# Second attention: which of a batch's 128 score tiles have their row sums taken by ScalarE, cut from 22 to 13

## The chip, the cores and the metric

One core of one Trainium2 chip runs the whole kernel. The metric is the device time of one execution in microseconds (us), the median of several runs; lower is better.

## What is computed

Two transformer-like blocks over x of shape (4, 1024, 128). The first has an attention with softmax over negative Euclidean distances and a mixture of experts. The change touches only the second block:

```python
xn = layernorm(x)
q, k, v = split(xn @ w_in.T + b_in)          # 16 heads of width 8
att = softmax(einsum('blhd,bmhd->blmh', q, k) / sqrt(8), axis=2)
opt = einsum('blmh,blhd->blhd', att, v)      # v is weighted by the sum of its own row of att
x = x + opt @ w_out.T + b_out + sqrt(real**2 + imag**2)   # real, imag: xn @ cos(..), xn @ sin(..)
```

So of every 1024 x 1024 score matrix the kernel needs only exp of each entry and the sum of each row.

## The kernel before, in words

The kernel has two long stages. In the first (to 996 us) the first attention and the experts run. In the second, from 996 us to the end, there are 4 batches x 16 heads x 8 row blocks = 512 score tiles of 128 rows x 1024 columns, 128 of them in a batch. A tile has a number s from 0 to 127 in its batch; `n` is its head counted over all batches and `i` its row block. Below, "tile 81" is s = 81.

Each tile goes through three engines.

- TensorE (PE) makes the scores into one of `RING` = 3 buffers of PSUM (`scores1`, L1211). It may fill a buffer when the exp of the tile three earlier has released it.
- ScalarE (ACT) takes exp of the tile into SBUF (`act_exp1`). There are 8 such places, in 4 tensors of two (`EX`), so tile s uses the place of tile s - 8. Before the exp of an even tile, ACT waits for the semaphore `summed` (L1226), until VectorE has folded every tile up to s - 7.
- The row sum of the tile is made in one of two ways. Mostly VectorE (DVE) does a fold (`dve_fold`, L1244): it adds the left and right half of the tile and writes out the row sum as an accumulator. For tiles for which `sum_by_act` is true, ACT makes the sum as part of the exp (`accum_out`, L1232, followed by a read of its accumulator), and DVE has nothing to do for that tile beyond waiting for its exp. The others are L1236.

`sum_by_act` before the change is true in batches 0 to 2 for s = 16, 21, 26, ..., 121, that is 22 tiles of a batch, and for the last two row blocks of the last four heads of batch 3 (8 tiles).

Beside its folds DVE does other work at fixed places of a batch. All of it stands in one queue, written out by hand in `fast(dve)`, so each item waits for everything ahead of it:

- s = 30: add the attention output (L1067); 31 to 38 and 39 to 46: one add per tile (L1074, L1083); 40: L1298
- 47 to 54 statistics (L1091); 55 variance; 57 to 64 normalise (L1099)
- 72: copy of the transposed tokens (L1114)
- 81: q out of PSUM (`dve_keep_q1`, L1128). GpSimd (POOL) waits for this and then splits q into three bf16 parts with four instructions (L520, L522, L524, L526)
- 90: k out of PSUM (`dve_keep_k1`, L1137). It releases the PSUM buffer `aux`, for which PE's value product waits (`pe_value1`, L1156, in PE's queue behind the scores of tile 97)
- 92, 94, 96, 98: DVE's own split of k (L1143, L1147, L1149, L1151)
- 100: the values out of PSUM (`dve_keep_v1`, L1165). This releases `aux` again; the first mix product waits for it (`pe_mix`, L1171, in PE's queue behind the scores of tile 108)
- 31, 63, 95, 127: the weights of four heads (`dve_weigh`, L1254 to L1259)

PE's queue is in order too, so the scores of tile 98 stand behind the value product's first part, and those of tile 109 behind the mix product's.
At tile 26, and in batches 1 to 3 at tile 36, PE puts four bias matmuls of 512 columns (L1047) between the scores of that tile and of the next.

Of the kernel before, what the change touches and what calls it, by code (L numbers as in the profile page):

```python
# [27 lines left out]
H = 16  # L28
HD = D // H
NT = N // P  # L30
HEADS = B * H
GROUP = 4
# [41 lines left out]


LAST_PARTS = [(0, 4), (4, 6), (6, 8)]


def sum_by_act(n, i):
    s = n % H * NT + i  # L80
    return n < HEADS - H and 12 <= s < 124 and s % 5 == 1 or n >= HEADS - GROUP and i >= LAST_PARTS[-1][0]

# [4 lines left out]
def tile_at(b, s):  # L89
    if b < B - 1 or s < LAST_GROUP:  # L90
        return b * H + s // NT, s % NT
    s -= LAST_GROUP
    lo, hi = next((lo, hi) for lo, hi in LAST_PARTS if s < GROUP * hi)
    head, i = divmod(s - GROUP * lo, hi - lo)
# [4 lines left out]
for tile_number in range(HEADS * NT):  # L99
    FOLDS.append(FOLDS[-1] + (not sum_by_act(*tile_at(*divmod(tile_number, H * NT)))))  # L100
# [85 lines left out]
def build(nc, d):  # L186
    with ExitStack() as ctx, ExitStack() as scores_ctx, ExitStack() as room:
# [1033 lines left out]
        def act_exp1(act, o, b, s):  # L1221
            (n, i), k = tile_at(b, s), s % NT
            tile = o.filled(act, ("qk1", n, i))
            if n:
                if k % 2 == 0:
                    act.wait_ge(summed, FOLDS[b * H * NT + s - NT + 2])  # L1226
            elif i == 0:
                act.wait_ge(pv_done, CHG * (GROUPS - 1) + CH)
            if sum_by_act(n, i):
                if n >= 2 * GROUP:  # L1230
                    act.wait_ge(w_done, n // GROUP - 1)
                nc.scalar.activation(EX[k // 2][:, k % 2, :], tile, ACT.Exp, scale=SCALE1,  # L1232
                                     accum_out=den[n // GROUP % 2][:, n % GROUP, i:i + 1]
                                     ).then_inc(o.release(("qk1", n, i)), 1)
            else:
                nc.scalar.activation(EX[k // 2][:, k % 2, :], tile, ACT.Exp, scale=SCALE1  # L1236
                                     ).then_inc(o.release(("qk1", n, i)), 1)

        def dve_fold(dve, o, b, s):
            (n, i), k = tile_at(b, s), s % NT  # L1240
            o.emptied(dve, ("qk1", n, i))
            if not sum_by_act(n, i):
                tile = EX[k // 2]
                nc.vector.scalar_tensor_tensor(  # L1244
                    out=tile[:, k % 2, 0:N // 2], in0=tile[:, k % 2, 0:N // 2], scalar=1.0,
                    in1=tile[:, k % 2, N // 2:N], op0=ALU.mult, op1=ALU.add,
                    accum_out=den[n // GROUP % 2][:, n % GROUP, i:i + 1]).then_inc(summed, 1)

        def dve_weigh(dve, u, part, number, sums_ready, count):

            side, b, blocks = u % 2, u // PER_BATCH, slice(*part)
            weights, sums_of = wsum[side][:, :, blocks], den[side][:, :, blocks]
            dve.wait_ge(sums_ready, count)
            nc.vector.reciprocal(weights, sums_of).then_inc(inv_done, 1)  # L1254
            dve.wait_ge(inv_done, number)
            nc.vector.tensor_tensor(weights, weights, sums_of, ALU.mult).then_inc(w_done, 1)
            dve.wait_ge(w_done, number)
            vals = V1[b][:, blocks, u % PER_BATCH * 32:(u % PER_BATCH + 1) * 32].rearrange("p t (h e) -> p t h e", e=HD)
            nc.vector.tensor_tensor(vals, vals, bcast(weights.rearrange("p h t -> p t h"), 3, HD), ALU.mult  # L1259
                                    ).then_inc(weighed, 1)  # L1260

        def dve_weigh_last(dve, number):
            lo, hi = LAST_PARTS[number]
            dve_weigh(dve, GROUPS - 1, (lo, hi), GROUPS + number, summed,
                      FOLDS[(B - 1) * H * NT + LAST_GROUP + GROUP * hi])
# [37 lines left out]
        def pe_turn_last(pe, o, number, slot):  # L1303
            lo, hi = LAST_PARTS[number]
            tile = o.begin(pe, ("fturn", B - 1, number), slot)
            pe.wait_ge(weighed, PER_BATCH * B + number)
            for t in range(lo, hi):
                mm = nc.tensor.transpose(tile[:, (t - lo) * P:(t - lo + 1) * P], V1[B - 1][:, t, :], ident)
                if t == hi - 3:
                    yield  # L1310
            mm.then_inc(o.fills(("fturn", B - 1, number)), 1)
            yield

        def dve_keep_last(dve, o, number):
            lo, hi = LAST_PARTS[number]
            tile = o.filled(dve, ("fturn", B - 1, number))
            nc.vector.tensor_copy(fatt[:, lo * P:hi * P], tile[:, 0:(hi - lo) * P]
                                  ).then_inc(o.release(("fturn", B - 1, number)), 1)

        def pe_project_last(pe, o, number, slot):  # L1320
            lo, hi = LAST_PARTS[number]
            tile = o.begin(pe, ("fwo", B - 1, number), slot)
            add_bias(tile, "bo1", hi - lo)
            yield
            o.emptied(pe, ("fturn", B - 1, number))
            for t in range(lo, hi):
                mm = nc.tensor.matmul(tile[:, (t - lo) * P:(t - lo + 1) * P], fatt[:, t * P:(t + 1) * P], late["wo1"],
                                      start=False, stop=(t == hi - 1))
                if t < hi - 1:
                    yield  # L1330
            mm.then_inc(o.fills(("fwo", B - 1, number)), 1)
            yield
# [984 lines left out]
```

## Time and profile before

| | us |
|---|---|
| median of 3 runs | 1486.84 |
| lowest and highest of them | 1486.05, 1487.32 |
| the profiled execution, as timed | 1486.19 |
| its span, first to last instruction | 1484.5 |
| second stage, from 996 us to the end | 488 |
| exp of tiles, ACT | 512 instructions |

The second stage begins at 996.2 us, and its batches begin at 996.2, 1114.8, 1234.2 and 1353.6 us. Batches 0, 1 and 2 follow the same pattern to within hundredths of a microsecond in the part that the argument uses, so one of them, batch 1, is read in detail. In the timeline views, each line is a merged group: start of the first instruction, microseconds from there to the end of the last, and what it is. ACT's instructions overlap in the trace (the next is shown as started before the one ahead has ended), so distances are best taken from end to end.

### The profile page before, as it was taken

How to read it: one execution, taken by the hardware profiler on the slowest of the kernel's cores; microseconds unless marked ns; L12 is line 12 of the kernel's file. 1: busy time of each engine (PE TensorE's matmuls, PEld its weight loads, DVE VectorE, ACT ScalarE, POOL GpSimd, SP SyncE). 2: the span in 40 equal slices, each digit the busy share in tenths (PEclk: the TensorE clock that was granted, in tenths of full speed). 3: DMA queues.
4: the chain of work that ended last, by engine and by line, in shares of the span. 5: the costliest groups of instructions: out<-in, count | busy, mean ns of one | idle time of the engine just before them, and what ended most of it. 6: DMA issues, size and time to landing. Idle time of an engine off the chain costs nothing.

```text
span 1484.5 us, 21370 instructions
## 1 busy us (share of the span) xinstructions
PE 1121.4 (76%) x7881; PEld 441.7 (30%) x7910; DVE 1245.5 (84%) x2236; ACT 1450.1 (98%) x792; POOL 413.7 (28%) x305
## 2 busy tenths in 40 slices
PE   5587786887887978878878774777677677776666
PEld 2123223243252442433424411232123222222212
DVE  7997978988989889789797787858898898988786
ACT  4899999999999999999999999999999999999998
POOL 5184460655503302123022130032123024022200
PEclk8598988999999999999999987899999999999999
DMA  4842644223242112121121420134033133021020
GB/s 130 240 131 61 177 127 124 52 57 84 79 135 69 51 43 53 43 56 52 43 66 30 95 74 18 32 107 87 27 112 84 27 112 83 27 91 48 21 70 20
DMA packets 104059, 112.71 MB, mean 76 GB/s; under 512 B 41722, under 2 KB 76026, under 8 KB 103946
## 3 DMA queue, kind: packets, MB, share of 16 engines
q1 hardware_dynamic: 98618, 99.47, 24.7%
q0 software_dynamic: 4464, 11.09, 2.7%
q8 instruction: 66, 1.08, 0.3%
q10 hardware_dynamic: 864, 0.69, 0.2%
q14 instruction: 47, 0.39, 0.1%
HBM read 66.52 MB, written 44.70 MB: 75 GB/s over the span
## 4 chain that ended last, share of the span: by engine, by line
ACT 69%; DVE 17%; issue 7%; PE 7%; DMA 1%; SPq 0%; DVEq 0%; ACTq 0%
ACT scores L719 25%; ACT scores L708 23%; ACT exp L1236 13%; DVE exp L1244 7%; DVE scores L683 6%; ACT exp L1232 3%; PE pvb L664 2%; ACT ht L969 1%; PE ring L649 1%; ACT L719 1%; ACT L708 1%; PE ring L426 1%; PE ring L930 1%; PE ring L1211 0%; DMA limit_full<-in_limit_full 0%
## 5 line engine op out<-in xcount | busy, mean ns | idle before, releaser
L683 DVE TENSOR_SCALAR scores<-ring 128x1024 f32<-128x1024 f32 x512 | 589.6, 1215 | 31.5 <-PE ring L649 31.3
L719 ACT ACTIVATE scores<-scores 128x8192 f32<-128x8192 f32 x64 | 445.8, 7021 | 0.2
L1236 ACT ACTIVATE exp<-ring 128x1024 f32<-128x1024 f32 x438 | 431.4, 1398 | 0.2
L708 ACT ACTIVATE scores<-scores 128x8192 f32<-128x8192 f32 x60 | 417.1, 7020 | 0.7 <-DVE scores L683 0.6
L1211 PE MATMUL ring<-stk 128*128 128x512 bf16 x995 | 299.5, 384 | 128.3 <-ACT exp L1236 106.6
L664 PE MATMUL pvb<-scores,val 128*9 128x256 f32 x4096 | 325.2, 392 | 89.9 <-ACT scores L719 44.0
L1244 DVE SCALAR_TENSOR_TENSOR exp<-exp 128x512 f32<-128x512 f32 x438 | 321.8, 757 | 62.1 <-ACT exp L1236 57.8
L649 PE MATMUL ring<-stk 64*128 64x512 bf16 x1024 | 210.3, 408 | 54.6 <-DVE scores L683 43.5
L1211 PEld LDWEIGHTS ring<-stk 128*128 128x128 bf16 x1024 | 65.7, 97 | 338.1 <-ACT exp L1236 241.8
L649 PEld LDWEIGHTS ring<-stk 64*128 64x128 bf16 x1024 | 49.8, 93 | 287.3 <-DVE scores L683 199.1
L664 PEld LDWEIGHTS pvb<-scores,val 128*9 128x9 f32 x4096 | 65.5, 89 | 219.4 <-issue 215.4
L704 POOL DMA_DIRECT2D att<-attg x32 | 25.2, 790 | 344.0 <-DVE attg L697 343.2
L1232 ACT ACTIVATE exp<-ring 128x1024 f32<-128x1024 f32 x74 | 101.1, 1369 | 0.2 <-PE ring L1211 0.2
L974 POOL TENSOR_TENSOR ht<-ht,gate 128x2464 f32<-128x2464 f32 x10 | 54.6, 5462 | 146.4 <-ACT ht L969 146.4
L930 PE MATMUL ring<-w,xjt 128*128 (+1 forms) x280 | 86.9, 469 | 1.2 <-DVE xjt L957 1.2
L672 PE MATMUL pvb<-fixed_full,ot 128*128 128x128 f32 x128 | 30.2, 320 | 55.0 <-DVE ot L688 55.0
L930 PEld LDWEIGHTS ring<-w,xjt 128*128 128x128 f32 x280 | 53.6, 195 | 30.2 <-issue 1.9
L976 POOL TENSOR_TENSOR gate<-gate,ht 128x2464 f32<-128x2464 f32 x10 | 54.6, 5457 | 0.8
L950 PE MATMUL ring<-w,ht 128*128 128x128 f32 (+3 forms) x420 | 49.4, 276 | 4.5 <-DVE ht L981 4.5
L950 PEld LDWEIGHTS ring<-w,ht 128*128 128x128 f32 (+1 forms) x420 | 47.7, 191 | 6.7 <-issue 4.2
L987 DVE COPY yj<-ring 128x896 f32<-128x896 f32 x10 | 10.9, 1092 | 42.0 <-PE ring L950 42.0
L962 DVE COPY ht<-ring 128x352 f32<-128x352 f32 x70 | 36.7, 525 | 10.9 <-PE ring L930 4.0
(252 smaller groups left out, 1178.8 us busy)
## 6 DMA issues: line engine op xcount, KB each, us to landing
stk<-stack SPq DMA_DIRECT2D x192, 192.0 KB, 2.9
stack<-qp SPq DMA_DIRECT2D x7, 768.0 KB, 4.4
stack<-kp SPq DMA_DIRECT2D x7, 768.0 KB, 5.7
xj<-xg SPq DMA_DIRECT2D x10, 448.0 KB, 4.2
yg<-yj POOLq DMA_DIRECT2D x10, 448.0 KB, 3.6
stack<-qp SPq DMA_DIRECT2D x7, 512.0 KB, 5.1
stack<-kp SPq DMA_DIRECT2D x7, 512.0 KB, 5.1
stk<-sum_rows SPq DMA_DIRECT2D x128, 24.0 KB
```

Source lines behind the costliest of these rows:

```text
L649: mm = nc.tensor.matmul(tile[:, cols], stk0[slot][side, K, j * P:(j + 1) * P], stk0[slot][side, Q, cols], start=True, stop=True)
L664: mm = nc.tensor.matmul(pvb[place % 2][32 * c:32 * c + VW, 0:256], val[place][:, j, :], S[place][:, j * N + c * 256:j * N + (c + 1) * 256] ...
L683: nc.vector.tensor_scalar(S[place][:, j * N:(j + 1) * N], tile, 1e-12, None, ALU.max).then_inc(o.release(("qk", group, place, j)), 1)
L708: nc.scalar.activation(S[place][:], S[place][:], ACT.Sqrt).then_inc(root_done, 1)
L719: nc.scalar.activation(S[place][:], S[place][:], ACT.Exp, scale=-1.0).then_inc(exp_done, 1)
L930: mm = nc.tensor.matmul(tile[:, side * 512:side * 512 + I], xjt[:, j * P:(j + 1) * P], weights_of(w13, e[j])[:, :, side, :].rearrange("p o ...
L950: mm = nc.tensor.matmul(tile[:, j * P:(j + 1) * P], ht[0:width, j, c * P:(c + 1) * P], weights_of(w2, e[j])[0:width, :, c, :].rearrange("p ...
L974: nc.gpsimd.tensor_tensor(h1, h1, gate[:, :, :], ALU.mult).then_inc(part_done, 1)
L1211: mm = nc.tensor.matmul(out[:, cols], stk1[place][:, Q, i * P:(i + 1) * P], stk1[place][:, K, cols], start=True, stop=True)
L1232: nc.scalar.activation(EX[k // 2][:, k % 2, :], tile, ACT.Exp, scale=SCALE1, accum_out=den[n // GROUP % 2][:, n % GROUP, i:i + 1]).then_in ...
L1236: nc.scalar.activation(EX[k // 2][:, k % 2, :], tile, ACT.Exp, scale=SCALE1).then_inc(o.release(("qk1", n, i)), 1)
L1244: nc.vector.scalar_tensor_tensor(out=tile[:, k % 2, 0:N // 2], in0=tile[:, k % 2, 0:N // 2], scalar=1.0, in1=tile[:, k % 2, N // 2:N], op0 ...
```

## The change

The rule of every fifth tile now holds only for tiles in three stretches of a batch. Of the 22 tiles of a batch (0 to 2) that ACT summed, 9 go to DVE: 31, 36, 41 (between 28 and 44) and 66, 71, 76, 81, 86, 91 (between 62 and 94). 13 stay with ACT. Over three batches 27 row sums move. The counts for which ACT and DVE wait (`FOLDS`) are computed from the same function and follow. Batch 3 is not changed, and nothing else moves.

```diff
 LAST_PARTS = [(0, 4), (4, 6), (6, 8)]
+DENSE = [(12, 28), (44, 62), (94, 124)]


 def sum_by_act(n, i):
     s = n % H * NT + i
-    return n < HEADS - H and 12 <= s < 124 and s % 5 == 1 or n >= HEADS - GROUP and i >= LAST_PARTS[-1][0]
+    dense = any(lo <= s < hi for lo, hi in DENSE)
+    return n < HEADS - H and dense and s % 5 == 1 or n >= HEADS - GROUP and i >= LAST_PARTS[-1][0]
```

## Rows read from the trace of the kernel before

**Rows 1.** The page: span, and busy time and share of each engine.
```profile
span 1484.5 us, 21370 instructions
PE 1121.4 (76%) x7881; PEld 441.7 (30%) x7910; DVE 1245.5 (84%) x2236; ACT 1450.1 (98%) x792; POOL 413.7 (28%) x305
```

**Rows 2.** ACT in order of time, batch 3, tiles summed by DVE only.
```profile
1412.12 56.14 ACT L1236 ACTIVATE exp<-ring 128x1024 f32<-128x1024 f32 x61
...
1412.12 2.06 ACT L1236 ACTIVATE exp<-ring 128x1024 f32<-128x1024 f32 x2
```

**Rows 3.** ACT in order of time, batch 1, tiles 81 to 86.
```profile
1190.47 1.46 ACT L1232 ACTIVATE exp<-ring 128x1024 f32<-128x1024 f32 x1
...
1191.47 4.21 ACT L1236 ACTIVATE exp<-ring 128x1024 f32<-128x1024 f32 x4
1195.09 1.51 ACT L1232 ACTIVATE exp<-ring 128x1024 f32<-128x1024 f32 x1
```

**Rows 4.** ACT, tiles 36 and 37 of batch 1, then of batch 3.
```profile
1148.73 1.10 ACT L1232 ACTIVATE exp<-ring 128x1024 f32<-128x1024 f32 x1
...
1149.93 1.02 ACT L1236 ACTIVATE exp<-ring 128x1024 f32<-128x1024 f32 x1
...
1393.47 1.25 ACT L1236 ACTIVATE exp<-ring 128x1024 f32<-128x1024 f32 x1
...
1394.82 1.02 ACT L1236 ACTIVATE exp<-ring 128x1024 f32<-128x1024 f32 x1
```

**Rows 5.** DVE in order of time, batch 1: folds of tiles 45 and 47.
```profile
1158.76 0.70 DVE L1244 SCALAR_TENSOR_TENSOR exp<-exp 128x512 f32<-128x512 f32 x1
...
1160.32 0.69 DVE L1244 SCALAR_TENSOR_TENSOR exp<-exp 128x512 f32<-128x512 f32 x1 [0.32 <-ACT exp L1236]
```

**Rows 6.** DVE, batch 1: q (tile 81), folds of tiles 83, 87 and 88.
```profile
1192.05 1.28 DVE L1128 TENSOR_SCALAR ysh<-aux,late_full 128x1024 f32<-128x1024 f32 x1 [0.30 <-ACT exp L1232]
...
1193.88 1.49 DVE L1244 SCALAR_TENSOR_TENSOR exp<-exp 128x512 f32<-128x512 f32 x1
...
1199.28 2.60 DVE L1244 SCALAR_TENSOR_TENSOR exp<-exp 128x512 f32<-128x512 f32 x1
...
1201.82 0.68 DVE L1244 SCALAR_TENSOR_TENSOR exp<-exp 128x512 f32<-128x512 f32 x1
```

**Rows 7.** POOL in order of time: first and last of the four splits of q.
```profile
1193.40 1.43 POOL L520 CAST qp<-ysh 128x1024 bf16<-128x1024 f32 x1 [22.46 <-DVE ysh L1128]
...
1198.88 2.45 POOL L526 TENSOR_TENSOR qp<-ysh,qp 128x1024 bf16<-128x1024 f32 x1
```

**Rows 8.** DVE, batch 1: k (tile 90), fold of tile 99, values (tile 100).
```profile
1203.65 1.27 DVE L1137 TENSOR_SCALAR yro<-aux,late_full 128x1024 f32<-128x1024 f32 x1
...
1213.06 0.69 DVE L1244 SCALAR_TENSOR_TENSOR exp<-exp 128x512 f32<-128x512 f32 x1
...
1214.28 1.23 DVE L1165 TENSOR_TENSOR V<-aux,late_rows 128x1024 f32<-128x1024 f32 x1
```

**Rows 9.** Stretches of batch 1: microseconds, DVE busy, granted clock, DMA.
```profile
1192.05:1201.82 9.77, 9.77 (x12) 1.00 0.07 22
1201.82:1213.06 11.24, 11.14 (x28) 1.00 0.44 158
```

**Rows 10.** ACT in order of time, batch 1: tiles 105, 106 and 108 with 109.
```profile
1212.64 1.70 ACT L1236 ACTIVATE exp<-ring 128x1024 f32<-128x1024 f32 x1
1213.84 1.42 ACT L1232 ACTIVATE exp<-ring 128x1024 f32<-128x1024 f32 x1
...
1215.76 2.33 ACT L1236 ACTIVATE exp<-ring 128x1024 f32<-128x1024 f32 x2
```

**Rows 11.** PE, batch 1: first value product, scores of tile 98, first mix product.
```profile
1204.98 0.71 PE L1156 MATMUL aux<-late_full,att_t 128*128 128x128 f32 x4 [0.23 <-DVE yro L1137]
1205.53 0.59 PE L1211 MATMUL ring<-stk 128*128 128x512 bf16 x2
...
1215.56 0.70 PE L1171 MATMUL aux<-cs,att_t 128*128 128x256 f32 x2 [0.56 <-DVE V L1165]
```

## The prediction

> **What bounds the kernel now.** I read the page first: ACT is busy 98% of the span, DVE 84% [rows 1]. That is an average, so next I read ACT in order of time where the change acts. In batch 3 61 exps in a row run without ACT summing anything. From the end of the second to the end of the last are 56.14 - 2.06 = 54.08 us for 59 steps, 0.9166 us each [rows 2]. ACT is back to back, and this is its pace. In batch 1 the exp of tile 81, which ACT sums, ends at 1190.47 + 1.46 = 1191.93 and that of tile 86, the next such, at 1196.60 [rows 3]: 4.67 us for five steps, against 5 x 0.9166 = 4.58. So **a row sum made by ACT costs 0.08 us**, and it falls behind the tile (the four exps between have their last end at 1195.68, 3.75 us after tile 81, where 4 steps are 3.67). The rest of the work of the stage is hidden behind this pace as long as PE and DVE keep up. Starts run ahead of ends in these rows, so a start that slips shows a gap and costs nothing until it comes later than 0.10 us before the end of the exp ahead. I take that bound from an exp started late, which takes 1.02 us [rows 4]: with 1.02 - 0.92 = 0.10 of overlap the pace still holds.
>
> The second thing to read is how far DVE is behind, because ACT may not write tile s (even) before tile s - 7 is folded. A fold takes 0.61 us from start to start when DVE is behind: from the fold of tile 99 over that of tile 100 to the values, 1213.06 to 1214.28 for two [rows 8]. In most of a batch DVE is quicker than ACT's pace. Between tiles 82 and 105 it isn't.
>
> **What the change removes.** 27 sums of ACT, nine in each of batches 0 to 2, at 0.08 us. One place gives nothing: tile 36 in batches 1 and 2. There the next exp waits for PE, which has bias matmuls to do. With ACT summing tile 36 (batch 1) the ends of 36 and 37 are 1149.83 and 1150.95, 1.12 us apart; in batch 3, where ACT doesn't sum it, they are 1394.72 and 1395.84, the same 1.12 us [rows 4]. So 25 sums pay: before tile 81 six in batch 0 (0.49 us), five in batches 1 and 2 (0.41 us each). Tiles 81, 86 and 91 I account for below, with what follows.
>
> **What it adds before tile 81: nothing.** Between 28 and 46 DVE has an add per tile beside its folds. Fold 45 starts at 1158.76, 0.39 us after its exp is there. With three more folds (3 x 0.61) and an ACT that is 3 x 0.08 us earlier it starts 0.39 + 1.83 + 0.24 = 2.5 us late. ACT would be held from 4.6 us on: the exp seven steps on ends 7 x 0.917 = 6.42 us after this one and starts 1.02 before its end, and a fold's sum is out 0.78 after its start (step 4), 6.42 - 1.02 - 0.78. After that, DVE is idle from time to time (0.32 us ahead of fold 47 [rows 5]) and skips tiles 46, 51, 56 and 61, so it has caught up before the normalisation at 57, and PE's transposes at 68 see it on time. The folds of 66, 71 and 76 go into idle time: today DVE waits for ACT before each next fold. Cover gone, each would cost 0.61 us.
>
> **From tile 81 to tile 109: the loss.** Let T be the end of exp 81 (1191.93 today).
> 1. *The q copy moves.* Today DVE takes q out at 1192.05, T + 0.12 [rows 6]. Now fold 81 stands ahead of it: it starts at T + 0.03 and the copy 0.61 later, T + 0.65. That is 0.53 us later. POOL waits for this copy: its four splits run from 1193.40 to 1201.33 [rows 7] and start 0.53 us later too.
> 2. *DVE crawls meanwhile.* During these 8 us DVE does one fold per POOL instruction: folds 83, 84, 85 and 87 start between 1193.88 and 1199.28 and two of them take 2.60 us; the next starts at 1201.82 [rows 6]. Without POOL four folds are 2.4 us. The pattern starts from the q copy, so I let it move as a whole, with 86 as the fourth fold in place of 87.
> 3. *Two more folds in the backlog.* 86 and 91 each push what follows by 0.61. So all DVE work from fold 92 on is 0.53 + 1.22 = 1.76 us later, counted from T. There is no idle time to take it: DVE is busy 9.77 of 9.77 us and then 11.14 of 11.24 [rows 9].
> 4. *ACT is held.* Fold 99 starts today at 1213.06, T + 21.13 [rows 8], and exp 106 starts right when its sum is out, 1213.84, 0.78 later, while exp 105 ends only at 1214.34 [rows 10]: the wait is there today, and free by 0.4 us. In the new kernel fold 99 starts at T + 22.89 and exp 106 at T + 23.67; it ends at T + 24.69 and exp 109, three steps and one ACT sum on, at T + 27.52.
> 5. *The same by another way.* The values leave PSUM today at 1215.51 [rows 8], the mix product has waited for that by 0.56 us [rows 11], and exp 109 starts at 1216.73, 1.22 after (the pair 108 and 109 ends at 1218.09 [rows 10]). In the new kernel the values are out at T + 25.34, exp 109 starts at T + 26.56 and ends at T + 27.58. Two waits agree to 0.06; I take the later one.
> Today exp 109 ends at T + 26.16. **The new kernel is 1.42 us later there**, and the two sums of 86 and 91 and that of 81 are already in it. On the way there are smaller holds (tile 94: fold 87 starts at T + 10.41 instead of being done; tile 98, below), and these are absorbed: the later wait sets the time.
>
> After tile 109 DVE skips 111, 116 and 121 as today and catches up, and the loads of the next batch's first head are not near the edge. Batch 3 has no changed tile.
>
> **The sum.** Batch 0: +1.42 - 0.49 = +0.93. Batches 1 and 2: +1.42 - 0.41 = +1.01 each. Together +2.96 us. The profiled execution has a span of 1484.5 and a time of 1486.19; it becomes 1487.5 and 1489.1. The median of the runs, 0.65 above that execution, becomes **1489.8**. Anything under 0.2% (3.0 us) can't be told from no change here, so the forecast stands just on that line, on the slow side of the old kernel.
>
> **The rule of the skill that promises a gain.** The trace shows ACT at 98% and everything else well below [rows 1]. The Trainium skill ("Perfetto Trace Analysis", Identifying the Most-Contended Engine) says to find the engine with the highest occupancy and relieve that one; by that rule this change should win. The rows on DVE between 82 and 106 speak against it: there DVE, not ACT, is the engine without slack. What the rule gives is the first rival.
>
> **Rivals.**
> - *Gain: the eight places of exps take up the backlog.* Then only the 25 paying sums count: 25 x 0.08 = 2.0 us less, 1484.8. The point from which it decides is fold 99: with exp 105 ending at T + 22.16, it must start by T + 21.28, and today it starts at T + 21.13. So 0.15 us of added backlog is free, and a single fold is 0.61. It would need idle time that rows 9 don't show. 0.06.
> - *The q copy's move costs nothing*, because POOL's splits catch a fold less or the pattern shifts into place. Then 1.22 instead of 1.76: per batch 1.42 - 0.53 = 0.89, and the sum is 3 x 0.89 - 1.31 = +1.4, 1488.2. 0.14.
> - *PE's wait adds up.* The value product waits 0.23 us for the k copy today [rows 11]; that copy (1203.65 [rows 8]) is 1.14 us later after folds 81 and 86. The scores of tile 98 are then made at T + 15.3 (today 1206.12, T + 14.2), where exp 98 should start at T + 14.9 at the latest. This 0.4 us is absorbed in my sum; if it isn't, 3 x 0.4 is on top: 1491.0. 0.14.
> - *A fold more is caught in each POOL chain.* A caught fold takes up to 2.54 us from start to start instead of 0.61 (1199.28 to 1201.82 [rows 6]): 3 x 1.9 on top, 1495.6. For it: the chain starts later against ACT, with DVE further behind. Against: there are four POOL instructions, and each lets one fold through. 0.07. The Trainium skill ("SBUF — State Buffer", Who interferes with whom) names the cause, one port pair held for a whole instruction by whichever of VectorE and GpSimd starts first, while the other fully blocks. The durations in rows 6 and 7 agree; the rule doesn't say who goes first after the move.
>
> **How the numbers follow.** The forecast has 0.59. Its own spread is 0.7 us (0.65 between profiled execution and median is the size of the scatter, and batches repeat to hundredths). Half of it lies over the line of 3.0 us. Slower: 0.30 + 0.14 + 0.07 = 0.51. Same: the other 0.29, and 0.14 + 0.06 with the gain rival, whose 0.13% is within the line: 0.49. Faster by over 0.2% would need more than all 27 sums give (2.2 us), so I take only 0.02 for it out of the 0.49. Range: the forecast and its two neighbours, 1487.7 to 1491.4, which holds 0.87 less their outer tails, about 0.8. Outside are the gain and the caught fold.
>
> **What would show it.** Right: exps of L1232 39 + 8 instead of 66 + 8; folds of L1244 465 instead of 438; the four POOL splits of batch 1 start 2.0 us after exp 81's end instead of 1.5; ACT starts near tiles 94, 98, 104 and 106 with an exp of 1.02 us behind a gap; tile 81 to 109 takes 27.6 us from end to end instead of 26.2; PE's wait ahead of L1156 above 1 us. Wrong: exps from 94 to 106 without gaps (gain), a q split that hasn't moved, or five folds of more than a microsecond between the q copy and tile 90.

## The result, and the profile after

| | before | after |
|---|---|---|
| median, us | 1486.84 | 1492.58 |
| lowest to highest of 7 runs | 1486.05 to 1487.49 | 1491.43 to 1492.88 |
| the profiled execution, as timed | 1486.19 | 1492.79 |
| its span | 1484.5 | 1491.1 |

The ratio is 1.0035, with a 95% interval of 1.0026 to 1.0044. The kernel became 5.7 us slower. The forecast was 3.0 us slower (1489.8) with a range up to 1491.4, so the direction was right, the size was about half of the measured one, and the measured time lies above the range.

The page of the changed kernel, in the lines that answer to [rows 1], and its groups of exps and folds:

```profile
span 1491.1 us, 21395 instructions
...
PE 1130.5 (76%) x7910; PEld 445.0 (30%) x7910; DVE 1260.0 (84%) x2290; ACT 1449.1 (97%) x765; POOL 414.5 (28%) x305
...
L1238 ACT ACTIVATE exp<-ring 128x1024 f32<-128x1024 f32 x465 | 438.3, 1310 | 5.2 <-PE ring L1213 3.7
...
L1246 DVE SCALAR_TENSOR_TENSOR exp<-exp 128x512 f32<-128x512 f32 x465 | 339.4, 752 | 55.3 <-ACT exp L1238 49.0
...
L1234 ACT ACTIVATE exp<-ring 128x1024 f32<-128x1024 f32 x47 | 56.6, 1207 | 1.2 <-PE ring L1213 0.8
```

27 sums have moved (465 folds, 47 sums of ACT). Line numbers are two higher than before. What is new is idle time of ACT ahead of its exps, 5.2 and 1.2 us, and its largest releaser is PE, not DVE. The kernel before shows 0.2 and 0.2 us:

```profile
L1236 ACT ACTIVATE exp<-ring 128x1024 f32<-128x1024 f32 x438 | 431.4, 1398 | 0.2
...
L1232 ACT ACTIVATE exp<-ring 128x1024 f32<-128x1024 f32 x74 | 101.1, 1369 | 0.2 <-PE ring L1211 0.2
```

**Where the time goes.** I compare the end of each exp with the same exp in the kernel before, counted from the end of the batch's first exp. The table gives the changed kernel less the one before in microseconds, for tile 112 and for four points on the way; a minus means that the changed kernel is ahead.

| up to the end of exp | batch 0 | batch 1 | batch 2 |
|---|---|---|---|
| 81 | -0.48 | -0.41 | -0.40 |
| 93 | -0.73 | -0.65 | -0.65 |
| 99 | +1.62 | +0.08 | +1.71 |
| 109 | +1.62 | +1.10 | +1.70 |
| 112 | +1.62 | +1.83 | +1.70 |

The three batches lose 5.15 us together. Nothing more is lost between tile 112 and the end of a batch, and batch 3 is as before. The profiled execution has another 0.94 us ahead of the second stage. In a second trace of the same kernel the second stage starts 0.66 us earlier than before, so that part is scatter between executions: over the twelve traces of this document, whose kernels are the same up to there, the stage starts between 995.2 and 997.4 us. The last 0.5 us of the difference in span (6.6 us) falls behind the last exp. Those are the last four matmuls of the kernel before, and of the changed one:

```profile
1481.08 0.71 PE L1327 MATMUL ring<-late_full,fatt 128*128 128x128 f32 x4
...
1487.19 1.19 PE L1329 MATMUL ring<-late_full,fatt 128*128 128x128 f32 x4
```

In the changed kernel the granted clock (the share of TensorE's full clock that it is given) is at 0.50 there, from 1486.6 us on; in the kernel before it falls at 1482.4 us, when PE is done. Seven of the twelve traces have 5.7 to 6.0 us behind the last exp and five 5.3 to 5.4; e7_quiet_sums below, the fastest kernel, is one of the seven. So this part stays out of the batch figures.

**What came out as forecast.** Below is DVE of the changed kernel in order of time, batch 1: q, folds 83, 86, 87 and 99, values. T, the end of exp 81, is 1194.09 here.

```profile
1194.74 1.28 DVE L1130 TENSOR_SCALAR ysh<-aux,late_full 128x1024 f32<-128x1024 f32 x1
...
1196.55 1.51 DVE L1246 SCALAR_TENSOR_TENSOR exp<-exp 128x512 f32<-128x512 f32 x1
...
1201.97 2.60 DVE L1246 SCALAR_TENSOR_TENSOR exp<-exp 128x512 f32<-128x512 f32 x1
...
1204.50 0.68 DVE L1246 SCALAR_TENSOR_TENSOR exp<-exp 128x512 f32<-128x512 f32 x1
...
1216.97 0.68 DVE L1246 SCALAR_TENSOR_TENSOR exp<-exp 128x512 f32<-128x512 f32 x1
...
1218.19 1.22 DVE L1167 TENSOR_TENSOR V<-aux,late_rows 128x1024 f32<-128x1024 f32 x1
```

And POOL's first split of q, then ACT's exps of tiles 106 and 109, of the same batch:

```profile
1196.09 1.43 POOL L522 CAST qp<-ysh 128x1024 bf16<-128x1024 f32 x1 [22.75 <-DVE ysh L1130]
...
1217.74 1.02 ACT L1234 ACTIVATE exp<-ring 128x1024 f32<-128x1024 f32 x1 [0.41 <-issue]
...
1220.72 1.02 ACT L1238 ACTIVATE exp<-ring 128x1024 f32<-128x1024 f32 x1
```

The q copy starts at T + 0.65 (1194.74 - 1194.09), the first split at T + 2.00, fold 87 at T + 10.41, fold 99 at T + 22.88, and the exps of 106 and 109 at T + 23.65 and T + 26.63. The prediction had 0.65, 2.0, 10.41, 22.89, 23.67 and 26.56. In batches 0 and 2 DVE's items stand at the same distances from T, fold 99 at 22.88 in both. In batch 1 tiles 81 to 109 take 27.66 us from end to end (forecast 27.6, before 26.2).

**What didn't.** In batch 1 another 0.73 us goes between tiles 109 and 112, and in batches 0 and 2 the whole loss comes by tiles 98 and 99. There exp 106 starts at T + 24.33 and T + 24.34, 0.7 us later than DVE's fold 99 would let it (T + 23.67), so in these two batches it isn't DVE's wait that sets the time. These are ACT's rows of tiles 98 and 99 in batch 0 and of tile 111 in batch 1:

```profile
1089.34 1.02 ACT L1238 ACTIVATE exp<-ring 128x1024 f32<-128x1024 f32 x1 [1.25 <-PE ring L1213]
...
1090.94 1.02 ACT L1238 ACTIVATE exp<-ring 128x1024 f32<-128x1024 f32 x1 [0.58 <-PE ring L1213]
...
1223.28 1.02 ACT L1234 ACTIVATE exp<-ring 128x1024 f32<-128x1024 f32 x1 [0.62 <-PE ring L1213]
```

All three wait for PE. PE in batch 0, in order of time, at the place of [rows 11]:

```profile
1087.23 1.22 PE L1158 MATMUL aux<-late_full,att_t 128*128 128x128 f32 x4 [1.31 <-DVE yro L1139]
1088.24 1.06 PE L1213 MATMUL ring<-stk 128*128 128x512 bf16 x2
1089.10 1.06 PE L1158 MATMUL aux<-late_full,att_t 128*128 128x128 f32 x4
...
1090.74 0.61 PE L1158 MATMUL aux<-late_full,att_t 128*128 128x128 f32 x4
```

PE waits 1.31 us for DVE's k copy (0.23 before), and then each group of four value matmuls takes 1.22 and 1.06 us where [rows 11] have 0.71, and 0.61 again from 1090.74 on. The stretches of 3.4 us at that place, in batches 0, 1 and 2, say why. The columns after the time are busy time (and instructions) of PE, PE's weight loads, DVE, ACT and POOL, then the granted TensorE clock, the DMA share and GB/s.

```profile
1085.30:1087.30 2.00, 0.67 (x3) 0.18 (x3) 2.00 (x6) 2.00 (x4) 0.00 (x0) 0.99 0.99 379
1087.30:1090.70 3.40, 3.40 (x12) 2.63 (x13) 3.40 (x10) 1.82 (x2) 0.00 (x0) 0.50 0.69 266
...
1220.40:1223.80 3.40, 3.40 (x9) 1.77 (x8) 3.40 (x13) 2.74 (x4) 0.00 (x0) 0.50 0.62 207
...
1329.60:1333.00 3.40, 3.40 (x13) 2.52 (x14) 3.40 (x10) 1.74 (x2) 0.00 (x0) 0.50 0.70 269
```

**The granted clock is at 0.50, that is 1.2 GHz instead of 2.4, for 3.4 us in each of the three batches**, right behind a stretch in which PE was busy for a third of the time or little more (0.67 of 2.00 us, 0.94 of 2.40, 0.69 of 2.00). In the kernel before it stays at 1.00 throughout batches 0 to 2 ([rows 9] show two of its stretches). A fall isn't new to it, though: in batch 3 it has one of 6.8 us from 1373.2 on, and the ends of exps 17 to 19, which lie in it, are 0.91 to 0.92 us apart, ACT's pace. The changed kernel has 10.2 us there, and its exps of batch 3 are those of the kernel before to 0.01 us. The slow stretch falls on the value product in batches 0 and 2 and on the mix product in batch 1, which is just where ACT loses time that the forecast doesn't have.

### The profile page after: what moved, and what is told of

The parts are those of the page before. It is cut to its first block, busy times and chain, and to the rows that moved or that the text cites. A ratio compares the mean times of both kernels' runs of the same rounds, so it can differ in the third digit from the quotient of the medians.

```text
span 1491.1 us, 21395 instructions
## 1 busy us (share of the span) xinstructions
PE 1130.5 (76%) x7910; PEld 445.0 (30%) x7910; DVE 1260.0 (84%) x2290; ACT 1449.1 (97%) x765; POOL 414.5 (28%) x305
## 4 chain that ended last, share of the span: by engine, by line
ACT 72%; issue 11%; DVE 10%; PE 3%; POOL 2%; DMA 1%; SPq 0%; DVEq 0%; ACTq 0%; POOLq 0%
ACT scores L721 28%; ACT scores L710 27%; ACT exp L1238 12%; DVE exp L1246 4%; DVE scores L685 4%; ACT ht L971 1%; ACT exp L1234 1%; ACT L721 1%; ACT L710 1%; POOL yro L1025 1%; PE ring L428 1%; PE pvb L666 1%; PE ring L1213 1%; DMA x<-in_x 0%; PE ring L651 0%
## 5 line engine op out<-in xcount | busy, mean ns | idle before, releaser
L1238 ACT ACTIVATE exp<-ring 128x1024 f32<-128x1024 f32 x465 | 438.3, 1310 | 5.2 <-PE ring L1213 3.7
L1213 PE MATMUL ring<-stk 128*128 128x512 bf16 x1024 | 308.5, 388 | 120.6 <-ACT exp L1238 106.2
L1246 DVE SCALAR_TENSOR_TENSOR exp<-exp 128x512 f32<-128x512 f32 x465 | 339.4, 752 | 55.3 <-ACT exp L1238 49.0
L1234 ACT ACTIVATE exp<-ring 128x1024 f32<-128x1024 f32 x47 | 56.6, 1207 | 1.2 <-PE ring L1213 0.8
L1188 POOL TENSOR_TENSOR at<-at 128x1024 f32<-128x1024 f32 x8 | 17.4, 2175 | 102.1 <-DVE at L1184 102.1
```

The lines of the kernel that those rows point to most:

```text
L1213: mm = nc.tensor.matmul(out[:, cols], stk1[place][:, Q, i * P:(i + 1) * P], stk1[place][:, K, cols], start=True, stop=True)
L1246: nc.vector.scalar_tensor_tensor(out=tile[:, k % 2, 0:N // 2], in0=tile[:, k % 2, 0:N // 2], scalar=1.0, in1=tile[:, k % 2, N // 2:N], op0 ...
```

## The experiments

The theory after the result: the loss has two parts, DVE's backlog as forecast (3 us), and a fall of TensorE's clock (2 us), brought about by ACT's holds and PE's waits for DVE. The rivals: the backlog alone costs 5 us, and the clock is harmless or chance; or the early sums cost something too.

Each kernel was timed in 5 to 11 executions, against executions of the kernel before. The edits below are against the changed kernel. The summary is in one table, with the ratio of the times and its 95% interval, and batch figures as above (end of exp 112, less the kernel before, from one trace of each kernel); a star marks a batch in which the clock fell between tiles 94 and 112.

| kernel | median, us (before) | ratio, interval | batches 0, 1, 2 |
|---|---|---|---|
| changed | 1492.58 (1486.84) | 1.0035 (1.0026 to 1.0044) | 1.62*, 1.83*, 1.70* |
| e0_again | 1492.24 (1487.16) | 1.0038 (1.0024 to 1.0051) | 1.75*, 2.09*, 1.50* |
| e1_late_sums | 1493.73 (1487.16) | 1.0043 (1.0029 to 1.0057) | 2.01*, 2.58*, 1.42 |
| e2_early_sums | 1486.35 (1487.16) | 0.9993 (0.9984 to 1.0002) | -0.23, -0.41, -0.41 |
| e3_pe_later | 1492.86 (1487.16) | 1.0035 (1.0022 to 1.0049) | 0.89*, 0.96, 0.96 |
| e9_pe_later2 | 1489.07 (1486.69) | 1.0016 (1.0007 to 1.0025) | 0.88, 0.96, 1.16* |
| e4_pe_waits | 1488.19 (1486.69) | 1.0011 (1.0002 to 1.0020) | 0.25, 0.26, 0.25 |
| e6_no81 | 1491.50 (1486.69) | 1.0027 (1.0018 to 1.0037) | 1.71*, 0.88, 2.04* |
| e10_pe_busy | 1490.02 (1486.88) | 1.0020 (1.0011 to 1.0029) | 1.04, 1.03, 1.03 |
| e7_quiet_sums | 1483.71 (1486.69) | 0.9979 (0.9970 to 0.9988) | -0.70, -0.73, -0.73 |
| e8_early_q | 1485.93 (1486.88) | 0.9991 (0.9982 to 1.0000) | -0.34, -0.26, -0.27 |

**The changed kernel again (e0_again).** No edit.

> The changed kernel once more, for a second trace. Theory (DVE backlog and TensorE clock): each of batches 0 to 2 again loses 1.6 to 1.8 us from its first exp to that of tile 112, 5.1 us together; in each of them the granted TensorE clock falls to 0.5 for 3.4 us right behind a PE wait for DVE of over 1 us. The 0.9 us that the first trace shows ahead of the second stage is scatter of the start and goes. Rival (the change costs something ahead of the second stage too): the start of the second stage is again 0.9 us later than in the kernel before.

The three falls of the clock are at the same places. The start of the second stage is 0.66 us earlier than before instead of 0.94 later: the rival falls. The batches lose 5.34 us together (5.1 expected), singly 1.50 to 2.09 where 1.6 to 1.8 was expected. Batch 0 has 0.38 us of its loss already at tile 27, which is scatter of the first head's work.

**Only the late sums (e1_late_sums).**

```diff
-DENSE = [(12, 28), (44, 62), (94, 124)]
+DENSE = [(12, 78), (94, 124)]
```

> Only tiles 81, 86 and 91 go to DVE; ACT keeps 31, 36, 41, 66, 71, 76. Theory: the whole loss sits here. Batches lose 1.42 us by the two waits and 0.5 to 0.7 by the clock, 6.0 us together plus 0.2, so 6.3 us slower than the kernel before. Rival (the early sums fill DVE up and cost something too): clearly less than the 5.7 us of the whole change.

The whole loss sits in tiles 81, 86 and 91: 6.6 us in the median (6.3 expected). Batch 2 is the clean case: the clock stays at 1.00 there, and it loses 1.42 us, the very term of the sum. Batches 0 and 1, with a fall, lose 2.01 and 2.58.

**Only the early sums (e2_early_sums).**

```diff
+DENSE = [(12, 28), (44, 62), (78, 124)]
```

> Only tiles 31, 36, 41, 66, 71 and 76 go to DVE; ACT keeps 81, 86, 91. Theory: pure gain of 0.08 us for each of 16 sums that pay (tile 36 of batches 1 and 2 doesn't), 1.3 us faster; clock 1.0 in all of batches 0 to 2. Rival (DVE's longer backlog between 31 and 55 costs): 0 or slower, with gaps of ACT between tiles 31 and 60.

In the trace they gain as reckoned, 0.41 us in batches 1 and 2 (five sums that pay), with no gap of ACT and the clock at 1.00; batch 0 had again lost 0.25 by tile 27 and then gained 0.48. The median is 0.8 us lower (1.3 expected), and the interval of the ratio includes no change, so the gain is read from the trace alone.

**PE's products later (e3_pe_later, then e9_pe_later2).** The changed kernel, with PE's two products later, so that DVE's backlog is the same and PE doesn't meet it.

```diff
-        Q1_AT, K1_AT, SPLIT1_AT, V1_AT, MIX_AT = 79, 88, (92, 94, 96, 98), 97, (108, 120)
+        Q1_AT, K1_AT, SPLIT1_AT, V1_AT, MIX_AT = 79, 88, (92, 94, 96, 98), 99, (111, 120)
```

> The changed kernel with PE's value product two tiles later (99 instead of 97) and the first mix product three later (111 instead of 108), DVE's two copies with them: DVE has the same backlog up to tile 99, but PE no longer waits for it. Theory (part of the loss is TensorE's clock, which falls when PE has waited long): granted clock stays 1.0, ACT is held at 94, 104 and 106 only, exp 106 starts at T + 23.7 with T the end of exp 81, and the kernel is 2.8 us slower than before instead of 5.7. Rival (the clock fall is chance or harmless, all loss is the backlog): no difference to the changed kernel, 5.7 us slower.

The median, 5.7 us above the kernel before, is the rival's figure, and taken alone it would have spoken for it. The trace says otherwise: up to tile 112 the batches lose 0.89, 0.96 and 0.96 us. In batch 0 the clock fell all the same, for 3.4 us from 1097.8, and cost nothing by tile 112. Then I had made a new wait. The first mix product's copy had moved to tile 117, and the second product at 120 waited for it. PE's waits for DVE in this kernel (us in total, times, longest):

```profile
PE aux L1173 <- DVE at L1184: 3.8, 3, 1.3
```

By tile 127 the losses are 1.40, 2.53 and 1.47, so the new wait cost 0.51 us in batches 0 and 2 and 1.57 in batch 1, where the clock fell right behind it (0.50 from 1231.0 to 1234.4). So I ran it again with the first mix product at 110.

```diff
+        Q1_AT, K1_AT, SPLIT1_AT, V1_AT, MIX_AT = 79, 88, (92, 94, 96, 98), 99, (110, 120)
```

> The changed kernel with the value product two tiles later (99) and the first mix product two tiles later (110); the second mix product stays at 120, where the run before it had given PE a new wait of 1.3 us. Theory (PE's long wait for DVE lowers the granted clock, which adds to the backlog's loss): no PE wait for DVE above 0.6 us, granted clock 1.0 throughout batches 0 to 2, each batch loses 0.9 to 1.0 us, 2.8 together: 2.8 us slower than before. Rival (the time is lost to the backlog in any case and comes out elsewhere): again 5 to 6 us slower.

PE has no wait for DVE in the list any more, and the batches lose 0.88, 0.96 and 1.16; 3.0 us in the trace, 2.4 us in the median. The expectation missed in one thing: in batch 2 the clock fell all the same, for 6.8 us from 1335.4. It cost only 0.2 us, at tile 111, though parts of the mix product stand in that stretch at half speed; here PE had not first waited for DVE:

```profile
1339.19 1.06 PE L1173 MATMUL aux<-cs,att_t 128*128 128x256 f32 x2
```

So long waits of PE for DVE aren't needed for the clock to fall; with e3_pe_later's batch 0 that makes two batches of six in which ACT's holds alone came before a fall. Both kernels also try the forecast's step 4 by itself, without the mix product's wait of step 5: exp 109 starts at T + 26.48 to 26.49 in all six batches, and step 4 gives T + 26.50 (its end at 27.52 less 1.02).

**Only PE's wait (e4_pe_waits).** The kernel before, no sum moved, the value product one tile earlier.

```diff
+DENSE = [(12, 124)]
...
+        Q1_AT, K1_AT, SPLIT1_AT, V1_AT, MIX_AT = 79, 88, (92, 94, 96, 98), 96, (108, 120)
```

> The kernel before with no sum moved, only the value product one tile earlier (96 instead of 97) so that PE waits 1.2 us for DVE's k copy where it waited 0.2. DVE's backlog at tile 99 is that of before. Theory (PE's wait alone brings the clock down): granted clock 0.5 for 3.4 us behind the wait in most of batches 0 to 2, ACT held near tiles 97 to 99, 0.5 to 1 us lost per batch, 1.5 to 3 us slower. Rival (the clock falls only together with ACT's holds, which thin out PE's work): clock stays 1.0 and the kernel is at most 0.6 us slower, the 0.2 us per batch that the later scores of tile 97 cost.

PE's wait grew as meant, and the stretches around it show the clock untouched, in batch 1 too (columns as above):

```profile
PE aux L1158 <- DVE yro L1139: 3.2, 3, 1.1
```

```profile
1080.00:1105.00 25.00, 18.51 (x77) 7.03 (x77) 23.65 (x58) 24.85 (x33) 2.42 (x1) 1.00 0.43 150
...
1320.00:1348.00 28.00, 20.08 (x84) 7.67 (x84) 26.19 (x59) 27.86 (x37) 4.30 (x3) 1.00 0.41 141
```

My theory in the form "PE's wait brings the clock down" falls: three waits of 1.1 us and no fall. 0.25 us per batch is lost at tile 97, by its late scores, as the rival said; the median's 1.5 us is above that, with an interval from 0.3 to 3.0 us that holds the trace's 0.8.

**86 and 91 without 81 (e6_no81).**

```diff
+DENSE = [(12, 84), (94, 124)]
```

> The change with tile 81 left to ACT: 31, 36, 41, 66, 71, 76, 86 and 91 go to DVE. Theory (fold 81 delays the q copy and with it POOL's splits by 0.53 us, and everything behind): DVE's items behind tile 91 are 1.22 instead of 1.76 us later, exp 109 ends 0.53 us earlier in each batch than in the changed kernel without the clock's part, so 0.4 to 0.5 us lost per batch; PE's wait for the k copy is 0.9 us. With the clock unchanged 1.4 us slower than before; if the clock falls as well, 0.5 to 0.7 more per batch. Rival (fold 81 costs nothing, the backlog does not depend on where the q copy stands): the same loss per batch as in the changed kernel.

The text on record lists tiles that this kernel doesn't move: by its edit only 86 and 91 go to DVE. Without the early gains, the theory's figure is 1.42 - 0.53 = 0.89 us per batch. Batch 1, where the clock stays up, loses 0.88. And in all three batches, whatever the clock did, fold 99 starts at T + 22.35, 0.53 us earlier than in the changed kernel. So fold 81 does cost 0.53 us, by moving the q copy. In batches 0 and 2 the clock fell, and they lose 1.71 and 2.04, 0.8 and 1.2 us more for the same DVE work.

**PE kept busy (e10_pe_busy).** The changed kernel with all its waits, but some scores made twice, with the same result.

```diff
             tile = o.begin(pe, ("qk1", n, i))
+            s = n % H * NT + i
+            if n < HEADS - H and any(lo <= s < hi for lo, hi in ((82, 87), (92, 97), (102, 108))):
+                scores1(tile, n % GROUP, i)
             scores1(tile, n % GROUP, i).then_inc(ring_full, 1)
```

> The changed kernel with all its waits, but PE makes the scores of tiles 82 to 86, 92 to 96 and 102 to 107 of batches 0 to 2 twice, which adds work in time it idles and changes no result. The value product still waits 1.2 us or more for DVE. Theory (the granted clock falls because ACT's holds and the waits for DVE thin out PE's work; the fall costs 0.5 to 1.1 us per batch on top of the backlog): clock 1.0 through batches 0 to 2 and 0.9 to 1.1 us lost per batch, 3 us slower than before. Rival (the wait itself is what brings the clock down, or the clock isn't what costs): falls or losses of 1.6 us and more as in the changed kernel, 5 us slower.

This run decides between the two. PE's waits for DVE are those of the changed kernel or longer, and the clock doesn't fall in any batch. The changed kernel's waits, this kernel's, and then the same three stretches:

```profile
PE aux L1158 <- DVE yro L1139: 3.9, 3, 1.3
...
PE aux L1173 <- DVE V L1167: 1.9, 3, 1.5
```

```profile
PE aux L1173 <- DVE V L1167: 4.4, 3, 1.5
PE aux L1158 <- DVE yro L1139: 3.9, 3, 1.3
```

```profile
1080.00:1105.00 25.00, 20.91 (x96) 9.58 (x98) 24.16 (x60) 23.83 (x30) 2.46 (x2) 1.00 0.44 150
1200.00:1227.00 27.00, 22.07 (x100) 9.70 (x100) 26.25 (x62) 25.82 (x34) 2.83 (x2) 1.00 0.41 139
1320.00:1348.00 28.00, 23.20 (x103) 9.92 (x103) 27.25 (x64) 26.82 (x34) 3.67 (x3) 1.00 0.39 134
```

The changed kernel has 0.93, 0.94 and 0.94 in the clock's column there:

```profile
1080.00:1105.00 25.00, 18.97 (x75) 7.91 (x72) 23.58 (x56) 22.98 (x30) 2.90 (x2) 0.93 0.43 150
1200.00:1227.00 27.00, 20.12 (x80) 8.46 (x78) 25.60 (x61) 25.17 (x31) 3.88 (x3) 0.94 0.40 139
1320.00:1348.00 28.00, 21.82 (x84) 8.76 (x82) 26.78 (x61) 25.97 (x33) 5.06 (x3) 0.94 0.41 139
```

With more work for PE, nothing removed and no wait for DVE shortened, the kernel is faster than the changed one: the batches lose 1.04, 1.03 and 1.03 us, 3.1 together, and the median is 3.1 us above the kernel before. Exp 106 starts at T + 23.66 to 23.67 and exp 109 at T + 26.55 to 26.56 in every batch, where the forecast had 23.67 and 26.56: with the clock up its sum comes out (2.96 us forecast; 3.1 measured, 0.1 of it in batch 0 by tile 27). (The two ratios, 1.0020 and 1.0035, have intervals that just overlap, 1.0029 against 1.0026. What separates the kernels beyond their traces is the mean granted clock of whole executions: 0.930 over the 7 of the changed kernel, 0.934 over the 11 of this one, 0.933 over the 21 of the kernel before beside it. Three falls of 3.4 us to half are 0.0034 of the span.)

**Two kernels that use what was learnt.** First, DVE takes the sums where it has room (e7_quiet_sums).

```diff
+DENSE = [(50, 62), (78, 110)]
```

> DVE takes the sums where it has room, ACT keeps 51, 56, 61 and 81 to 106: 13 tiles of each of batches 0 to 2 move (16, 21, 26, 31, 36, 41, 46, 66, 71, 76, 111, 116, 121), 34 of them at places where ACT sets the pace. Theory: 34 x 0.08 = 2.8 us faster than before, clock 1.0. Rival (DVE's backlog from 28 to 64 grows far enough that the normalisation is late for PE's transposes at 68): a gap of ACT near tiles 71 to 74 and no gain.

It is **faster than both: 1483.71**, 3.0 us below the kernel before it was measured with (2.8 expected). By tile 127 the batches gain 0.86, 0.89 and 0.89 us. Its exps summed by DVE, and its PE's waits for DVE, which are those of the kernel before [rows 11]:

```profile
L1238 ACT ACTIVATE exp<-ring 128x1024 f32<-128x1024 f32 x477 | 454.3, 1436 | 0.6
```

```profile
PE aux L1173 <- DVE V L1167: 1.7, 3, 0.6
PE aux L1158 <- DVE yro L1139: 0.7, 3, 0.2
```

39 sums moved, 12 more than in the change, and ACT idles 0.6 us ahead of these exps instead of 5.2. Second, tile 81 moved too and the q projection three tiles earlier (e8_early_q).

```diff
+DENSE = [(50, 62), (84, 110)]
...
+        Q1_AT, K1_AT, SPLIT1_AT, V1_AT, MIX_AT = 76, 88, (92, 94, 96, 98), 97, (108, 120)
```

> ACT keeps only 51, 56, 61 and 86 to 106, and q is projected three tiles earlier (76 instead of 79), so that POOL's splits block DVE three tiles earlier and DVE has three more tiles to catch up before its own split of k. Theory (the loss comes from POOL's splits and DVE's split of k following closely): tile 81 may go to DVE too without a hold of ACT, clock 1.0, 37 x 0.08 = 3.0 us faster than before. Rival (the q product comes too early for PE, which then waits for DVE's copy of the transposed tokens): ACT held near tile 77, PE waits over 0.5 us there, and gain of 2 us or less.

The gain is 0.95 us in the median (the interval of the ratio ends at 1.0000), and neither had the cause right. PE waits for the token copy as the rival said (by 0.44 us), and in batches 1 and 2 the exp of tile 77 starts 1.37 us after that of 76 instead of the 0.90 of e7_quiet_sums, but that costs only 0.02 us from end to end:

```profile
1184.53 1.10 PE L1122 MATMUL aux<-att_t,late_full 128*128 128x512 f32 x2 [0.44 <-DVE att_t L1116]
```

What costs is tile 90, where ACT is held by DVE: with q earlier, the fold caught by POOL's last split is 83 (2.61 us instead of 0.68), and the exp of 90 needs its place. ACT's row of tile 90:

```profile
1198.62 1.02 ACT L1238 ACTIVATE exp<-ring 128x1024 f32<-128x1024 f32 x1 [0.42 <-DVE exp L1246]
```

That takes back 0.53 us in each batch. The clock stays up and ACT isn't held behind tile 92 any more, as wanted.

## Why the prediction was right about DVE and wrong about PE

**What bounds the kernel, what the change removes, and the early tiles: right.** A sum of ACT is worth 0.08 us: by the end of exp 81 the batches have gained 0.48, 0.41 and 0.40 (forecast 0.49, 0.41, 0.41), so tile 36 gives nothing in batches 1 and 2. The early folds fit in (e2_early_sums): fold 45 starts 2.2 us behind its exp, 2.5 forecast, and ACT isn't held.

**Steps 1 to 5, the backlog: right for DVE, and for ACT where the clock stays up.** In batch 1 the q copy and all that follows up to exp 106 land within 0.02 us of the forecast, exp 109 within 0.07. (In step 3, 0.53 + 1.22 is 1.75 and not 1.76; nothing hangs on it.) With the clock up the term of 1.42 is measured as 1.42 (e1_late_sums, batch 2), and its part from fold 81, 0.53, as 0.54 (1.42 less 0.88 of e6_no81, batch 1). The folds of 1.51 and 2.60 us are there again, one for each of POOL's instructions, as in [rows 6]; that is in line with the exclusive lock of which the Trainium skill tells ("SBUF — State Buffer", Who interferes with whom).

**The sum: wrong, by a term that wasn't in it.** The step that failed is the one that calls the holds on the way, that of tile 98 above all, absorbed, because "the later wait sets the time". The sum went from waits to time as if PE worked at the same pace behind a longer wait. I had put PE's wait down as a rival, priced it at the length of the wait, and found it absorbed. With the clock up that is so: in e10_pe_busy tile 98 is held by 0.4 us, and exp 109 comes when DVE's wait lets it. In the changed kernel the value matmuls take 1.06 to 1.22 us at a clock of 0.50 instead of 0.61 to 0.71, tiles 98 and 99 of batches 0 and 2 lose 2.0 us together, and DVE's wait, at T + 23.67, is no longer the later one. In batch 1 the same befalls the mix product. What I left out is that less work of PE in a stretch can cost it its clock. The kernel before has the granted clock at 1.00 all through this part [rows 9], and I read that as a constant and not as something that the change could touch, though the same trace has a fall in batch 3. The missing term is 5.15 less 3.1 (e10_pe_busy) = 2.05 us in the trace, 0.6 to 0.8 us in each batch, and 5.7 less 3.1 = 2.6 us in the medians. Put into the sum it gives 1486.84 + 2.96 + 2.05 = 1491.9; the median was 1492.58, and the 0.5 us behind the last exp is of the size of the rest.

**The range** went up to 1491.4, for a PE wait that adds up without the clock. The measured time lies above it. The rival "PE's wait adds up" had the right engine and the wrong mechanism: the wait itself costs 0.25 us (e4_pe_waits). The rival of a gain fell at the point that it named, and the fifth caught fold doesn't appear.

**What stays open.** What exactly brings the clock down isn't settled. PE waits of 1.1 us without holds of ACT: no fall in three batches (e4_pe_waits). Holds of ACT without PE waits: two in six (e9_pe_later2, e3_pe_later up to tile 112). Both: six in six for the change, two in three each in e1_late_sums and e6_no81. Both with added PE work: none in three. A thin stretch of PE isn't enough by itself: PE is busy for 0.39 of 2.00 us at 1203.6 in e4_pe_waits and for 0.57 of 2.00 at 1336.7 in e10_pe_busy, less than ahead of the falls in the changed kernel, and the clock stays at 1.00. So both take part, most likely, and I can't say which stretch of PE's work counts. Nor do the runs say why the same work has a fall in one batch and none in the next.

## What to carry to other kernels

Work given to an engine that idles on average is free only where its queue has slack behind it; read the lag of that engine tile by tile, and look for the point in the queue from which it never idles again until its result is needed. Three sums of nine in each batch (81, 86 and 91) made the whole loss here, because they stood just ahead of the stretch in which DVE is blocked by POOL's instructions and then has its own split to do. And if a change makes TensorE idle more in a stretch, ask whether its clock holds: a granted clock of 1.00 in the profile of before is a state that the change can end, and here it stayed at 1.00 when PE was given useless work.

## What the runs showed of the hardware that I had not expected

- In batches 0 to 2 the granted clock fell from 1.00 to 0.50 for 3.4 us (once 6.8), in the changed kernel behind stretches in which PE was busy for a third of the time or little more (0.67 of 2.00 us before the fall at 1087.3), in the middle of a stage where PE is otherwise busy around three quarters of the time. Four value matmuls then take 1.06 us instead of 0.61.
- Making 16 tiles' scores twice in each of three batches (e10_pe_busy) took 2 us off the three batches of the changed kernel.
- How much a fall costs depends on where PE stands when it comes: nothing in batch 3 of the kernel before and in batch 0 of e3_pe_later, 0.2 us where PE had no wait for DVE ahead of it (e9_pe_later2, batch 2), about 1.1 us more than in the other batches where it came right behind PE's wait ahead of a mix product (e3_pe_later, batch 1).
